# Conditioned residual block on one core: masks in a ring of six slots, and the second step's x tiles spread over 32 matrices

## Chip, core and metric

The kernel runs on one core of one Trainium2 chip. The metric is the device time of one execution in microseconds (us); the time of a kernel is the median of its runs. All arithmetic is on 32-bit floats. TensorE products are made three times, in split form (high and low parts), so that they come out near full precision.

## What is computed

```python
# x: 8 x 256 x 1024, mask: 8 x 1024 x 1024 of 0 and 1, W: 1024 x 1024
output = jnp.einsum('bsi,oi->bso', x, W) + b
sign = (2 * mask - 1)
diff = jnp.einsum('bsi,bio->bso', x, sign)
x = x + output + diff * coeff[:, None, None]
# then a gated feed-forward layer with low-rank adapters chosen by an index for each batch,
# down(silu(gate(x)) * up(x)), and x = x + that
```

The first part (here: stage 0) is what the change touches. For each of the 8 batches it is one product of x with a matrix of its own: W + identity + coeff * (2 * mask - 1). The feed-forward layer takes the other seven eighths of the time.

## The kernel before

**Steps and matrices.** The batches are handled in two steps s (`BLOCKS`) of four. In stage 0 the 1024 outputs are eight row tiles o, and each pair (batch b of four, row tile o) has one matrix of 128 x 1024. That is 64 matrices, numbered m = 0 to 63 here (`chunks`), and TensorE does 24 matmuls on each (`stage0`, L1245 to L1261): eight k tiles times three parts (high x high, high x low, low x high). Two matrices fill one bank of PSUM, and the bank is one tile q of 128 x 512 of the result.

**How a matrix is made.** SP loads its mask (`mask_dma`, L421) into `m_raw`, a ring of `S_RING` = 4 slots of 512 KB. ScalarE turns it into signs times coeff in place (`sign`, L638 to L643). VectorE adds the tile of W (`form_matrix`, L899 to L908), to which it has once for each row tile added the identity (L905). ScalarE rounds the sum into `m_hi` (`matrix_hi`, L645), VectorE puts the remainder into `m_lo` (`matrix_lo`, L910), and both are rings of four slots as well. A mask is loaded into a slot again when `matrix_lo` of four matrices earlier is done. `matrix_hi(m)` waits until TensorE is done with matrix m - 4.

**How x is made.** x is 32 tiles of 128 x 512, each split by ScalarE into a high part (`x_hi`) and by VectorE into a low part (`x_lo`). The 16 tiles of step 0 go to places of their own (`x_first`) at the start. The 16 tiles of step 1 (j = 16 to 31) go through `x_in`, a ring of `XIN_RING` = 4 slots, while step 0 is computed.

**Queues.** The order on each engine is written out by hand, as a loop over m with one body for each engine:

- SP (L475 to L481): the tile of W if m opens a row tile (`w_dma`, two slots, waits for the last matrix of the row tile before last), then mask m, then for m = 8 to 23 one x tile of step 1.
- ScalarE (L841 to L849), here "iteration m": for odd m the eviction of the finished tile (`finish_x1`), `sign(m + 5)`, `matrix_hi(m + 4)`, and for m = 2 to 17 `x_hi` of one tile of step 1.
- VectorE (L1178 to L1184), iteration m: `form_matrix(m + 5)`, `matrix_lo(m + 4)`, and for m = 2 to 17 `x_lo` of the same tile.
- GpSimd stores each finished tile of x1 to memory (L565 to L567), from a ring of three.

Each waits in its order, so what is behind a late `x_hi` on ScalarE is late too, and VectorE's next step with it.

**Start.** Masks 0 to 3 have slots free at once. Masks 4 to 7 are issued behind the 16 tiles of `x_first`. ScalarE and VectorE put matrix 4's sign and sum between the splits of tiles 11 and 12.

**Order of the row tiles.** Step 0 takes the halves of row tiles 0 and 1 in the order (0, 0), (1, 0), (0, 1), (1, 1), so that TensorE can go on before the second half of x has come. Step 1 takes them as (0, 0), (0, 1), (1, 0), (1, 1). Stage 0 ends when TensorE has done matrix 63; SP's loads of x1 for the next stage wait for that.

Of the kernel before, what the change touches and what calls it, by code (L numbers as in the profile page):

```python
# [7 lines left out]
P = 128  # L8
B, S, H, F, ADAPTERS, RANK = 8, 256, 1024, 2752, 16, 16
LORA_SCALE = 0.5  # L10
BLOCKS, HALVES = 2, 2
N = HALVES * S
HT = H // P
# [9 lines left out]
TR = 3 * R2  # L23
DR = 2 * RANK

S_RING = 4
G_RING, D_RING = 4, 8
G_RAW, D_RAW = 7, 14
OT_RING, FX_RING, LW_RING, X1_RING, XIN_RING = 3, 6, 2, 3, 4

PRODUCTS = ["p1", "p5", "p6", "p3", "p7", "p2", "p4"]
FIRST_PRODUCTS = ["p1", "p2", "p5", "p6", "p3", "p7", "p4"]
# [10 lines left out]

def first_stage_order():

    tiles = [(0, o, h) for o, h in [(0, 0), (1, 0), (0, 1), (1, 1)] + [(o, h) for o in range(2, HT) for h in range(2)]]
    return tiles + [(1, o, h) for o in range(HT) for h in range(2)]


def pe_order():  # L50
# [96 lines left out]
def build(nc, x, mask, coeff, w0, bias, wgu, wgu_half, wd, wd_left, a_gu, a_down, b_gu, b_down, idx, ident, own,  # L147
# [16 lines left out]
    with ExitStack() as ctx:  # L164
        def sb(stack, name, shape, dt):
            return stack.enter_context(nc.sbuf_tensor(name, shape, dt))
# [4 lines left out]
        def sems(name, n):  # L171
            return [sem(f"{name}{i}") for i in range(n)]
# [11 lines left out]

        with ExitStack() as first:
            xs = [sb(first, f"xs{s}", [P, HT * 2, 2 * N], f32r) for s in range(BLOCKS)]
            m_raw = sb(first, "m_raw", [P, S_RING, H], f32)
            m_hi = sb(first, "m_hi", [P, S_RING, H], f32r)
            m_lo = sb(first, "m_lo", [P, S_RING, H], f32r)
            w_in = sb(first, "w_in", [P, 2, H], f32)  # L190
            x_in = sb(first, "x_in", [P, XIN_RING, N], f32)
            x1_out = sb(first, "x1_out", [P, X1_RING, N], f32)
# [81 lines left out]
        x0_loaded, x_loaded = sems("x0_loaded", 2 * HT), sems("x_loaded", XIN_RING)  # L274
        xh_ready, xl_ready = sem("xh_ready"), sem("xl_ready")
        w_loaded, w_ident = sems("w_loaded", 2), sem("w_ident")
        m_loaded = sems("m_loaded", S_RING)
        sign_ready, m_ready, m_hi_ready, m_lo_ready = sem("sign_ready"), sem("m_ready"), sem("m_hi_ready"), sem("m_lo_ready")
        x1_made = sem("x1_made")
        x1_stored = sems("x1_stored", X1_RING)  # L280
# [130 lines left out]
        def _(sp):  # L411
            def x_dma(j):
                s, h, k = j // (2 * HT), j // HT % 2, j % HT
                if j < 2 * HT:
                    sp.dma_start(x_first[:, j, :], x[s, h, k, :, :]).then_inc(x0_loaded[j], 16)
                    return
                n = j - 2 * HT
                if n >= XIN_RING:
                    sp.wait_ge(xl_ready, j - XIN_RING + 1)
                sp.dma_start(x_in[:, n % XIN_RING, :], x[s, h, k, :, :]).then_inc(x_loaded[n % XIN_RING], 16)  # L420

            def mask_dma(m):
                s, o, b = chunks[m]
                if m >= S_RING:
                    sp.wait_ge(m_lo_ready, m - S_RING + 1)
                sp.dma_start(m_raw_i[:, m % S_RING, :], mask[4 * s + b, o, :, :]).then_inc(m_loaded[m % S_RING], 16)

            def w_dma(w):
                if w >= 2:
# [42 lines left out]
            mask_dma(3)  # L472
            for j in range(HT, 2 * HT):
                x_dma(j)
            for m in range(S_RING, len(chunks)):  # L475
                s, o, b = chunks[m]
                if s * HT + o >= 2 and b == 0:
                    w_dma(s * HT + o)
                mask_dma(m)
                if 8 <= m < 8 + 2 * HT:  # L480
                    x_dma(2 * HT + m - 8)  # L481

            sp.wait_ge(pe_done, done["s", first_half_end])
            for s in range(BLOCKS):
# [149 lines left out]
        def _(act):  # L634
            def copy(o, i):
                return nc.scalar.activation(o, i, ACT.Copy)  # L636

            def sign(m):  # L638
                s, o, b = chunks[m]
                act.wait_ge(m_loaded[m % S_RING], 16 * (m // S_RING + 1))  # L640
                nc.scalar.activation(m_raw[:, m % S_RING, :], m_raw_i[:, m % S_RING, :], ACT.Identity,
                                     bias=ncoeff[:, 4 * s + b:4 * s + b + 1], scale=coeff2[:, 4 * s + b:4 * s + b + 1]
                                     ).then_inc(sign_ready, 1)  # L643

            def matrix_hi(m):  # L645
                act.wait_ge(m_ready, m + 1)
                if m >= S_RING:
                    act.wait_ge(pe_done, done["s", m - S_RING])
                copy(m_hi[:, m % S_RING, :], m_raw[:, m % S_RING, :]).then_inc(m_hi_ready, 1)

            def x_hi(j):
                s, h, k = j // (2 * HT), j // HT % 2, j % HT
                if s == 0:
                    act.wait_ge(x0_loaded[j], 16)
                    src = x_first[:, j, :]
                else:
                    n = j - 2 * HT
                    if n == 0:
                        act.wait_ge(xl_ready, 2 * HT)
                    act.wait_ge(x_loaded[n % XIN_RING], 16 * (n // XIN_RING + 1))  # L660
                    src = x_in[:, n % XIN_RING, :]
                copy(xs[s][:, 2 * k, h * N:(h + 1) * N], src).then_inc(xh_ready, 1)
# [178 lines left out]
            for m in range(len(chunks)):  # L841
                if m % 2:
                    finish_x1(m // 2)
                if m + 5 < len(chunks):
                    sign(m + 5)
                if m + 4 < len(chunks):
                    matrix_hi(m + 4)
                if 2 <= m < 2 + 2 * HT:
                    x_hi(2 * HT + m - 2)  # L849

                if m == len(chunks) - 3:
                    for key in plan.items[:G_RING]:
                        prep(key)
# [35 lines left out]
        def _(dve):  # L889
            def sub(o, a, b):  # L890
                return nc.vector.tensor_tensor(o, a, b, ALU.subtract)  # L891

            def add(o, a, b):
                return nc.vector.tensor_tensor(o, a, b, ALU.add)  # L894
# [4 lines left out]
            def form_matrix(m):  # L899
                s, o, b = chunks[m]  # L900
                w = s * HT + o
                if b == 0:
                    dve.wait_ge(w_loaded[w % 2], 16 * (w // 2 + 1))
                    tile = w_in[:, w % 2, o * P:(o + 1) * P]
                    add(tile, tile, ident_sb[:, :]).then_inc(w_ident, 1)  # L905
                    dve.wait_ge(w_ident, w + 1)
                dve.wait_ge(sign_ready, m + 1)
                add(m_raw[:, m % S_RING, :], m_raw[:, m % S_RING, :], w_in[:, w % 2, :]).then_inc(m_ready, 1)  # L908

            def matrix_lo(m):  # L910
                dve.wait_ge(m_hi_ready, m + 1)
                sub(m_lo[:, m % S_RING, :], m_raw[:, m % S_RING, :], m_hi[:, m % S_RING, :]).then_inc(m_lo_ready, 1)

            def x_lo(j):
                s, h, k = j // (2 * HT), j // HT % 2, j % HT
                dve.wait_ge(xh_ready, j + 1)
                src = x_first[:, j, :] if s == 0 else x_in[:, (j - 2 * HT) % XIN_RING, :]
                cols = slice(h * N, (h + 1) * N)
                sub(xs[s][:, 2 * k + 1, cols], src, xs[s][:, 2 * k, cols]).then_inc(xl_ready, 1)
# [258 lines left out]
            for m in range(len(chunks)):  # L1178
                if m + 5 < len(chunks):
                    form_matrix(m + 5)  # L1180
                if m + 4 < len(chunks):
                    matrix_lo(m + 4)
                if 2 <= m < 2 + 2 * HT:
                    x_lo(2 * HT + m - 2)  # L1184

                if m == len(chunks) - 3:
                    make_first(plan.groups[0])
                    for key in plan.items[:G_RING]:
                        prep(key)
# [44 lines left out]
        def _(pe):  # L1234
# [10 lines left out]
            def stage0(m):  # L1245
                s, o, b = chunks[m]
                q, slot = m // 2, m % S_RING
                if m % 2 == 0 and q >= 4:
                    pe.wait_ge(x1_made, q - 3)
                pe.wait_ge(m_lo_ready, m + 1)  # L1250
                cols, dst = slice(b * S, (b + 1) * S), ps[q % 4][:, m % 2 * S:(m % 2 + 1) * S]
                for k in range(HT):
                    if (s, o) == (0, 0) or m == chunk_at[s, 0, 0]:
                        pe.wait_ge(xl_ready, 2 * HT * s + HT * (1 if s else b // 2) + k + 1)
                    elif (s, o, b) == (1, 0, 2) and k == 0:
                        pe.wait_ge(xl_ready, 4 * HT)
                    w = slice(k * P, (k + 1) * P)
                    mm(dst, m_hi[:, slot, w], xs[s][:, 2 * k, cols], start=k == 0, stop=False)  # L1258
                    mm(dst, m_hi[:, slot, w], xs[s][:, 2 * k + 1, cols], start=False, stop=False)  # L1259
                    end = mm(dst, m_lo[:, slot, w], xs[s][:, 2 * k, cols], start=False, stop=k == HT - 1)  # L1260
                end.then_inc(pe_done, 1)  # L1261
# [204 lines left out]
```

## Time and profile before

| | |
|---|---|
| median of three runs | 1719.38 us (1717.9 to 1721.31) |
| profiled execution, its own time | 1717.66 us |
| its span | 1715.9 us |
| TensorE matmul busy | 1586.7 us, 92% of the span |
| VectorE busy | 1284.7 us, 75% |
| ScalarE busy | 780.2 us, 45% |
| DMA, mean over the span | 190 GB/s, 325.23 MB |
| chain that ended last, by engine | PE 80%, DVE 8%, DMA 6%, ACT 2%, the rest 4% |

PE is TensorE, PEld its weight loads, DVE VectorE, ACT ScalarE, POOL GpSimd, SP the engine that issues most transfers. The engines' numbers are busy time within one profiled execution. The chain is followed back from the last instruction, at each step to what released it. Stage 0 is the first 217 us of the span, where TensorE's matmuls are those of L1258 to L1260.

### The profile page before, as it was taken

What the parts mean: (1) busy time and instruction counts of PE and PEld (TensorE: products, weight loads), DVE (VectorE), ACT (ScalarE), POOL (GpSimd) and SP (SyncE); (2) the same over time, 40 slices, a digit from 0 to 9 for tenths busy, and PEclk for the clock granted to TensorE, in tenths of its full rate; (3) what the DMA queues carried; (4) which work ended last, traced back from release to release, by engine and by line L of the source; (5) the groups of instructions that cost most, each with busy time, mean ns of one, the idle gap of its engine ahead of it and who ended that gap; (6) DMA issues with size and microseconds to landing.
All of it is one profiled execution on the core that took longest, in us unless ns stands there. A gap on an engine that the chain in (4) does not pass through costs nothing.

```text
span 1715.9 us, 23054 instructions
## 1 busy us (share of the span) xinstructions
PE 1586.7 (92%) x7502; PEld 1322.9 (77%) x7502; DVE 1284.7 (75%) x2250; ACT 780.2 (45%) x1426; POOL 344.2 (20%) x653
## 2 busy tenths in 40 slices
PE   6899948999999999969999579999999999699995
PEld 6899936888888888758888458888888888488884
DVE  7888857777777777668888877777677777688886
ACT  7888744444444444423333344444444444233321
POOL 0010121222222222161201011222222221511100
PEclk9999979999999999989999889999999999899998
DMA  8887672444444444698752734444444445996622
GB/s 302 295 281 278 239 235 95 144 145 144 145 144 145 144 145 144 198 397 282 249 200 74 246 113 133 146 146 149 144 147 146 147 144 164 379 335 230 224 65 98
DMA packets 134662, 325.23 MB, mean 190 GB/s; under 512 B 19216, under 2 KB 41872, under 8 KB 134544
## 3 DMA queue, kind: packets, MB, share of 16 engines
q0 software_dynamic: 58528, 188.39, 32.6%
q1 hardware_dynamic: 76016, 135.37, 23.9%
q8 instruction: 61, 1.00, 0.2%
q14 instruction: 57, 0.47, 0.1%
HBM read 231.42 MB, written 92.27 MB: 189 GB/s over the span
## 4 chain that ended last, share of the span: by engine, by line
PE 80%; DVE 8%; DMA 6%; ACT 2%; issue 2%; SPq 1%; POOL 1%; DVEq 0%; ACTq 0%; POOLq 0%
PE ps L1243 41%; PE ps L1239 28%; PE ps L1258 2%; PE ps L1260 2%; PE ps L1259 2%; PE ps L1346 2%; DMA fx<-x_scratch 2%; DMA x_in<-in_x 2%; DMA op_d<-operand_scratch 1%; DVE lo L891 1%; DVE acc L894 1%; DVE op_b L891 1%; DVE m_raw L894 1%; DVE m_lo L891 1%; DMA m_raw<-in_mask 1%
## 5 line engine op out<-in xcount | busy, mean ns | idle before, releaser
L636 ACT ACTIVATE hi<-raw 128x512 fp32r<-128x512 f32 (+1 forms) x598 | 309.4, 519 | 310.6 <-PE ps L1243 177.0
L1243 PE MATMUL ps<-op_b,hi 128*128 128x512 f32 x1360 | 422.1, 392 | 8.0 <-ACT u2c L636 6.2
L891 DVE TENSOR_TENSOR lo<-raw,hi 128x512 fp32r<-128x512 f32 (+2 forms) x646 | 338.5, 531 | 110.1 <-ACT hi L636 108.6
L1239 PE MATMUL ps<-op_b,hi 128*128 128x512 f32 x1056 | 333.6, 398 | 18.8 <-DVE op_b L891 18.8
L1243 PEld LDWEIGHTS ps<-op_b,hi 128*128 128x128 f32 x1360 | 256.6, 189 | 64.4 <-ACT u2c L636 7.1
L1243 PE MATMUL ps<-op_b,lo 128*128 128x512 f32 x680 | 266.8, 392 | 0.0
L894 DVE TENSOR_TENSOR acc<-acc,ps 128x512 f32<-128x512 f32 x312 | 212.1, 685 | 70.6 <-PE ps L1243 39.5
L1239 PEld LDWEIGHTS ps<-op_b,hi 128*128 128x128 f32 x1056 | 202.2, 192 | 64.4 <-issue 18.2
L1243 PE MATMUL ps<-op_d,hi 128*128 128x512 f32 x640 | 206.3, 404 | 29.5 <-DVE acc L894 28.3
L518 POOL DMA_DIRECT2D operand_scratch<-ot x140 | 75.5, 539 | 665.9 <-DVE ot L891 659.3
L1239 PE MATMUL ps<-op_b,lo 128*128 128x512 f32 x528 | 208.4, 395 | 0.0
L1258 PE MATMUL ps<-xs,m_hi 128*128 128x256 f32 x512 | 149.5, 292 | 23.3 <-DVE m_lo L891 22.0
L1243 PEld LDWEIGHTS ps<-op_d,hi 128*128 128x128 f32 x640 | 119.8, 193 | 64.3 <-DVE acc L894 38.4
L531 POOL DMA_DIRECT2D b_in<-in_b_gu x264 | 134.5, 510 | 94.0 <-DVE lw L891 74.2
L1239 PE MATMUL ps<-op_d,hi 128*128 128x512 f32 x480 | 149.2, 392 | 1.0 <-DMA op_d<-operand_scratch 0.8
L891 DVE TENSOR_TENSOR ot<-a,ot 128x512 fp32r<-128x512 f32 x124 | 85.5, 690 | 85.3 <-ACT ot L636 85.3
L1243 PEld LDWEIGHTS ps<-op_b,lo 128*128 128x128 f32 x680 | 128.4, 189 | 27.1
L1260 PE MATMUL ps<-xs,m_lo 128*128 128x256 f32 x512 | 148.1, 289 | 0.0
L1259 PE MATMUL ps<-xs,m_hi 128*128 128x256 f32 x512 | 148.1, 289 | 0.0
L891 DVE TENSOR_TENSOR raw<-raw 128x512 f32<-128x512 f32 (+1 forms) x246 | 137.1, 557 | 3.0
L1243 PE MATMUL ps<-op_d,lo 128*128 128x512 f32 x320 | 127.5, 398 | 0.0
L1258 PEld LDWEIGHTS ps<-xs,m_hi 128*128 128x128 f32 x512 | 101.5, 198 | 25.1 <-DVE m_lo L891 22.5
(120 smaller groups left out, 2232.8 us busy)
## 6 DMA issues: line engine op xcount, KB each, us to landing
operand_scratch<-ot POOLq DMA_DIRECT2D x140, 512.0 KB, 3.9
op_d<-operand_scratch POOLq DMA_DIRECT2D x140, 512.0 KB, 11.2
raw<-in_wgu SPq DMA_DIRECT2D x168, 256.0 KB, 4.1
m_raw<-in_mask SPq DMA_DIRECT2D x64, 512.0 KB, 4.7
raw<-in_wd SPq DMA_DIRECT2D x160, 128.0 KB, 4.2
fx<-x_scratch SPq DMA_DIRECT2D x64, 256.0 KB, 3.8
b_in<-in_b_gu POOLq DMA_DIRECT2D x264, 32.0 KB, 2.3
w_in<-in_w SPq DMA_DIRECT2D x16, 512.0 KB, 4.8
```

Of the source, the lines that this page charges most:

```text
L518: pool.dma_start(dst, ot[:, 2 * slot:2 * slot + 2, :].rearrange("p a n -> p (a n)")).then_inc(ot_stored[slot], 16)
L531: pool.dma_start(b_in[c % 2][r:r + RANK, b // 2 * 2:b // 2 * 2 + 2, :], b_gu[ds(adapter[b], 1), :, :, 2 * P * c:2 * P * (c + 1)].rearrange ...
L636: return nc.scalar.activation(o, i, ACT.Copy)
L891: return nc.vector.tensor_tensor(o, a, b, ALU.subtract)
L894: return nc.vector.tensor_tensor(o, a, b, ALU.add)
L1239: return mm(dst, weight, v, start=start, stop=stop)
L1243: return mm(dst, weight, v, start=False, stop=stop, skip_group_check=True)
L1258: mm(dst, m_hi[:, slot, w], xs[s][:, 2 * k, cols], start=k == 0, stop=False)
L1259: mm(dst, m_hi[:, slot, w], xs[s][:, 2 * k + 1, cols], start=False, stop=False)
L1260: end = mm(dst, m_lo[:, slot, w], xs[s][:, 2 * k, cols], start=False, stop=k == HT - 1)
L1346: end = mm(ps[6 + half][:, :], lw_ap(key, half), ot[:, i, :], start=f == 0 and i == slot, stop=False)
```

## The change

Five edits, all in stage 0:

1. `m_raw` gets a ring of its own, `M_RING` = 6, so a mask is loaded when `matrix_lo` of six matrices earlier is done. `m_hi` and `m_lo` stay at four.
2. `XIN_RING` goes from 4 to 2.
3. The x tiles of step 1 are loaded after every second mask (m = 8, 10, .. 38) and split in every second iteration (m = 2, 4, .. 32).
4. At the start mask 4 is issued between the `x_first` tiles 11 and 12, mask 5 behind tile 15; the loop begins at mask 6.
5. Step 1 takes its first two row tiles in the same interleaved order as step 0, and TensorE waits for x tile by tile in the first matrix of each half of a row tile 0.

```diff
-S_RING = 4
+S_RING, M_RING = 4, 6
-OT_RING, FX_RING, LW_RING, X1_RING, XIN_RING = 3, 6, 2, 3, 4
+OT_RING, FX_RING, LW_RING, X1_RING, XIN_RING = 3, 6, 2, 3, 2
@@ def first_stage_order():
-    tiles = [(0, o, h) for o, h in [(0, 0), (1, 0), (0, 1), (1, 1)] + [(o, h) for o in range(2, HT) for h in range(2)]]
-    return tiles + [(1, o, h) for o in range(HT) for h in range(2)]
+    tiles = [(0, 0), (1, 0), (0, 1), (1, 1)] + [(o, h) for o in range(2, HT) for h in range(2)]
+    return [(s, o, h) for s in range(BLOCKS) for o, h in tiles]
@@
-            m_raw = sb(first, "m_raw", [P, S_RING, H], f32)
+            m_raw = sb(first, "m_raw", [P, M_RING, H], f32)
@@ mask_dma (sign, matrix_hi, form_matrix and matrix_lo use m % M_RING for m_raw likewise)
-                if m >= S_RING:
-                    sp.wait_ge(m_lo_ready, m - S_RING + 1)
+                if m >= M_RING:
+                    sp.wait_ge(m_lo_ready, m - M_RING + 1)
@@ SP's order
             for j in range(HT, 2 * HT):
                 x_dma(j)
-            for m in range(S_RING, len(chunks)):
+                if j == HT + 3:
+                    mask_dma(4)
+            mask_dma(5)
+            for m in range(M_RING, len(chunks)):
                 s, o, b = chunks[m]
                 if s * HT + o >= 2 and b == 0:
                     w_dma(s * HT + o)
                 mask_dma(m)
-                if 8 <= m < 8 + 2 * HT:
-                    x_dma(2 * HT + m - 8)
+                if m % 2 == 0 and 0 <= m - 8 < 4 * HT:
+                    x_dma(2 * HT + (m - 8) // 2)
@@ ScalarE's loop (VectorE's likewise, with x_lo)
-                if 2 <= m < 2 + 2 * HT:
-                    x_hi(2 * HT + m - 2)
+                if m % 2 == 0 and 0 <= m - 2 < 4 * HT:
+                    x_hi(2 * HT + (m - 2) // 2)
@@ stage0 on TensorE
-                    if (s, o) == (0, 0) or m == chunk_at[s, 0, 0]:
-                        pe.wait_ge(xl_ready, 2 * HT * s + HT * (1 if s else b // 2) + k + 1)
-                    elif (s, o, b) == (1, 0, 2) and k == 0:
-                        pe.wait_ge(xl_ready, 4 * HT)
+                    if o == 0 and b % 2 == 0:
+                        pe.wait_ge(xl_ready, 2 * HT * s + HT * (b // 2) + k + 1)
```

## Rows read from the trace of the kernel before

**Rows 1.** TensorE's matmuls in time: start, us, operation, idle before it and releaser

```profile
31.52 0.39 PE L1258 MATMUL ps<-xs,m_hi 128*128 128x256 f32 x1 [3.17 <-DVE m_lo L891]
...
42.99 0.39 PE L1258 MATMUL ps<-xs,m_hi 128*128 128x256 f32 x1 [1.09 <-DVE m_lo L891]
...
57.50 0.39 PE L1258 MATMUL ps<-xs,m_hi 128*128 128x256 f32 x1 [2.68 <-DVE m_lo L891]
...
72.06 0.39 PE L1258 MATMUL ps<-xs,m_hi 128*128 128x256 f32 x1 [2.69 <-DVE m_lo L891]
...
96.10 0.35 PE L1258 MATMUL ps<-xs,m_hi 128*128 128x256 f32 x1 [0.55 <-DVE m_lo L891]
...
214.25 0.28 PE L1258 MATMUL ps<-xs,m_hi 128*128 128x256 f32 x1
```

**Rows 2.** Waits from 28 to 98 us, TensorE's then ScalarE's: total, times, longest

```profile
PE ps L1258 <- DVE m_lo L891: 11.4, 6, 3.2
...
ACT xs L636 <- DMA x_in<-in_x: 12.7, 6, 3.6
```

**Rows 3.** Busy time by stretch: PE, PEld, DVE, ACT, POOL; then PEclk, DMA share, GB/s

```profile
32.00:34.00 2.00, 2.00 (x12) 2.00 (x11) 2.00 (x3) 2.00 (x3) 0.00 (x0) 0.50 0.84 291
44.00:54.00 10.00, 10.00 (x85) 10.00 (x85) 8.24 (x10) 7.27 (x11) 0.54 (x1) 1.00 0.96 346
56.00:58.00 2.00, 0.50 (x4) 0.50 (x5) 2.00 (x4) 2.00 (x3) 0.00 (x0) 1.00 0.06 23
43.00:101.00 58.00, 50.81 (x401) 50.02 (x402) 49.10 (x53) 48.65 (x58) 4.86 (x9) 0.97 0.80 282
101.00:145.00 44.00, 44.00 (x369) 44.00 (x368) 36.82 (x36) 37.51 (x40) 3.78 (x7) 1.00 0.81 280
```

**Rows 4.** ScalarE in time, from 53 to 57 us

```profile
53.18 0.67 ACT L669 ACTIVATE x_out<-ps,bias_sb 128x512 f32<-128x512 f32 x1
53.75 1.23 ACT L641 ACTIVATE m_raw<-m_raw,ncoeff,coeff 128x1024 f32<-128x1024 int32 x1
54.88 1.04 ACT L636 ACTIVATE m_hi<-m_raw 128x1024 fp32r<-128x1024 f32 x1
55.83 0.62 ACT L636 ACTIVATE xs<-x_in 128x512 fp32r<-128x512 f32 x1
56.35 1.23 ACT L641 ACTIVATE m_raw<-m_raw,ncoeff,coeff 128x1024 f32<-128x1024 int32 x1
```

**Rows 5.** VectorE in time, from 58 to 61 us

```profile
57.96 1.22 DVE L894 TENSOR_TENSOR m_raw<-m_raw,w_in 128x1024 f32<-128x1024 f32 x1
59.10 1.22 DVE L891 TENSOR_TENSOR m_lo<-m_raw,m_hi 128x1024 fp32r<-128x1024 f32 x1
60.23 0.69 DVE L891 TENSOR_TENSOR xs<-x_in,xs 128x512 fp32r<-128x512 f32 x1
60.84 1.22 DVE L894 TENSOR_TENSOR m_raw<-m_raw,w_in 128x1024 f32<-128x1024 f32 x1
```

**Rows 6.** VectorE's group for W plus identity, first 217 us: busy, mean ns

```profile
L894 DVE TENSOR_TENSOR w_in<-w_in,ident_sb 128x128 f32<-128x128 f32 x16 | 4.6, 285 | 3.9 <-DMA ident_sb<-in_ident 3.9
```

**Rows 7.** Transfers to landing: masks' median of stage 0, `x_in` min/median/max

```profile
m_raw<-in_mask SPq DMA_DIRECT2D x64, 512.0 KB, 4.7
...
DMA to landing us min/median/max: 3.8/5.5/6.5
```

**Rows 8.** The start in time, from 24 to 39 us: ScalarE, VectorE, SP, ScalarE

```profile
24.28 1.25 ACT L641 ACTIVATE m_raw<-m_raw,ncoeff,coeff 128x1024 f32<-128x1024 int32 x1 [1.03 <-DMA m_raw<-in_mask]
...
25.55 1.23 DVE L894 TENSOR_TENSOR m_raw<-m_raw,w_in 128x1024 f32<-128x1024 f32 x1 [0.73 <-ACT m_raw L641]
...
30.35 0.33 SPq L431 DMA_DIRECT2D w_in<-in_w  x1
...
31.86 0.43 SPq L420 DMA_DIRECT2D x_in<-in_x  x1
...
38.13 0.63 ACT L636 ACTIVATE xs<-x_in 128x512 fp32r<-128x512 f32 x1 [3.58 <-DMA x_in<-in_x]
```

More of the change, by code:

```diff
@@ L276, in build @@
         w_loaded, w_ident = sems("w_loaded", 2), sem("w_ident")
-        m_loaded = sems("m_loaded", S_RING)
+        m_loaded = sems("m_loaded", M_RING)
         sign_ready, m_ready, m_hi_ready, m_lo_ready = sem("sign_ready"), sem("m_ready"), sem("m_hi_ready"), sem("m_lo_ready")
@@ L423, in mask_dma @@
                 s, o, b = chunks[m]
-                if m >= S_RING:
-                    sp.wait_ge(m_lo_ready, m - S_RING + 1)
-                sp.dma_start(m_raw_i[:, m % S_RING, :], mask[4 * s + b, o, :, :]).then_inc(m_loaded[m % S_RING], 16)
+                if m >= M_RING:
+                    sp.wait_ge(m_lo_ready, m - M_RING + 1)
+                sp.dma_start(m_raw_i[:, m % M_RING, :], mask[4 * s + b, o, :, :]).then_inc(m_loaded[m % M_RING], 16)
             def w_dma(w):
@@ L639, in sign @@
                 s, o, b = chunks[m]
-                act.wait_ge(m_loaded[m % S_RING], 16 * (m // S_RING + 1))
-                nc.scalar.activation(m_raw[:, m % S_RING, :], m_raw_i[:, m % S_RING, :], ACT.Identity,
+                act.wait_ge(m_loaded[m % M_RING], 16 * (m // M_RING + 1))
+                nc.scalar.activation(m_raw[:, m % M_RING, :], m_raw_i[:, m % M_RING, :], ACT.Identity,
                                      bias=ncoeff[:, 4 * s + b:4 * s + b + 1], scale=coeff2[:, 4 * s + b:4 * s + b + 1]
@@ L648, in matrix_hi @@
                     act.wait_ge(pe_done, done["s", m - S_RING])
-                copy(m_hi[:, m % S_RING, :], m_raw[:, m % S_RING, :]).then_inc(m_hi_ready, 1)
+                copy(m_hi[:, m % S_RING, :], m_raw[:, m % M_RING, :]).then_inc(m_hi_ready, 1)
             def x_hi(j):
@@ L907, in form_matrix @@
                 dve.wait_ge(sign_ready, m + 1)
-                add(m_raw[:, m % S_RING, :], m_raw[:, m % S_RING, :], w_in[:, w % 2, :]).then_inc(m_ready, 1)
+                add(m_raw[:, m % M_RING, :], m_raw[:, m % M_RING, :], w_in[:, w % 2, :]).then_inc(m_ready, 1)
             def matrix_lo(m):
                 dve.wait_ge(m_hi_ready, m + 1)
-                sub(m_lo[:, m % S_RING, :], m_raw[:, m % S_RING, :], m_hi[:, m % S_RING, :]).then_inc(m_lo_ready, 1)
+                sub(m_lo[:, m % S_RING, :], m_raw[:, m % M_RING, :], m_hi[:, m % S_RING, :]).then_inc(m_lo_ready, 1)
             def x_lo(j):
@@ L1182, in _ @@
                     matrix_lo(m + 4)
-                if 2 <= m < 2 + 2 * HT:
-                    x_lo(2 * HT + m - 2)
+                if m % 2 == 0 and 0 <= m - 2 < 4 * HT:
+                    x_lo(2 * HT + (m - 2) // 2)
                 if m == len(chunks) - 3:
```

## The prediction

> **What bounds the kernel now.** I read the windows first, to see where TensorE is not full in stage 0; then its matmuls in time, for the first one behind each gap; then the waits of TensorE and of what releases it; last the order on ScalarE and VectorE. TensorE is full from 101 us on (369 matmuls in 44 us, clock 1.00) but not from 43 to 101 us (50.81 of 58 us busy, clock 0.97) [rows 3]. So the place to look is the first 101 us, where the second step's x tiles are loaded and split. Behind a gap stand the matmuls at 31.52, 42.99, 57.50, 72.06 and 96.10 us (and one at 86.6 us); they open matrices 4, 7, 11, 15, 22 and 19 [rows 1]. All were released by `matrix_lo`, 11.4 us in six waits [rows 2]. VectorE was late because ScalarE was, and ScalarE stood still 12.7 us in six waits for an `x_in` tile [rows 2]. The reader should see a period: about 14.5 us from gap to gap (42.99, 57.50, 72.06), which is four matrices, and every fourth matrix brings a tile of W.
>
> Why is an x tile late, when its ring has four slots? Not for lack of slots. SP issues it behind its mask, and mask m waits for `matrix_lo(m - 4)`, which VectorE does in iteration m - 8. ScalarE needs the tile in iteration m - 6. Two iterations are 5.8 us, and the tile takes 3.8 to 6.5 us to land, 5.5 at the median [rows 7]; with W's 512 KB ahead it is always at the long end.
>
> The full pace: matrices 22 to 63 start from 96.10 to 214.25 us [rows 1], 118.15 / 41 = 2.882 us each. From matrix 7 (42.99) to matrix 63 (214.25) it takes 171.26 us, where 56 matrices at full pace are 161.4. That leaves **9.9 us** to be had behind matrix 7: four gaps, plus matmuls at half clock behind one of them.
>
> **Masks in six slots.** Mask m now waits for `matrix_lo(m - 6)`, in iteration m - 10, and `sign(m)` is in iteration m - 5: five iterations, 14.4 us, against a median landing of 4.7 us [rows 7]. The x tile behind it is issued in iteration m - 10 and needed in m - 6: four iterations, 11.5 us, against at most 6.5 us [rows 7]. The ring of two for `x_in` adds a wait: tile i waits for `x_lo` of tile i - 2, which is also in iteration m - 10, just behind the `matrix_lo` that the mask waited for. Queued behind that wait on SP are only later masks, themselves not due for four iterations or more. It costs nothing, as long as a landing takes less than four iterations. `w_dma` ahead of mask m waits for the sum of matrix m - 5, also in iteration m - 10, so it holds up nothing either.
>
> **Splits over 32 matrices.** Start to start, ScalarE's steps are 0.57 (eviction), 1.13 (sign), 0.95 (high part), 0.52 (x) [rows 4]; VectorE's are 1.14 (sum), 1.13 (low part), 0.61 (x) [rows 5], and 0.285 for W once in four [rows 6]. Four matrices before: ScalarE 4 x (1.13 + 0.95 + 0.52) + 2 x 0.57 = 11.5, VectorE 4 x 2.88 + 0.3 = 11.8; TensorE needs 4 x 2.882 = 11.5. So both were at TensorE's pace or over it even with no transfer late, and could never catch up. After: ScalarE 11.5 - 2 x 0.52 = 10.5, VectorE 11.8 - 2 x 0.61 = 10.6. They gain 0.9 us on TensorE in each four matrices. Matrices 18 to 33, which had no split and now have one in two, keep this margin, so the added work there is hidden by TensorE; if that cover were gone it would cost at most 8 x 0.61 = 4.9 us.
>
> **DMA.** In four matrices go four masks and a W tile of 0.524 MB each, two stores of x1 (0.524 MB together) and now two x tiles (0.524 MB) for four: 3.67 MB in 11.53 us, 318 GB/s. The trace moved 346 GB/s over the ten busy us from 44 to 54, and 23 GB/s from 56 to 58, while TensorE had nothing [rows 3]. The mean of 282 over 43 to 101 us therefore holds idle stretches and is no ceiling. I take 346 as the nearest row for what the queue can do, and keep 282 for a rival. More of SP's transfers are now in flight beside GpSimd's stores, which have three slots and so 17 us each; I cost that at nothing.
>
> The Trainium skill's page "DMA: Bandwidth & Descriptors" (section "Issuing engines are not separate DMA queues") says that transfers of all issuing engines run on the same 16 DMA engines and interleave. That speaks against a deeper ring, since masks sent early delay the x tiles and the stores. The trace agrees so far as the `x_in` tile takes up to 6.5 us behind other transfers against 3.8 at its shortest. Taken at its worst it is the first rival below.
>
> **The start.** ScalarE waited 1.03 us for mask 4 and VectorE then 0.73 us for ScalarE [rows 8]. With mask 4 issued four tiles earlier both waits go; the bytes up to tile 15 are the same, so that tile comes when mask 4 came before (24.3 us), and it is split near 26 us. VectorE has no other slack, so everything is 0.73 us earlier: matrix 4 at 30.8 instead of 31.52. The gap ahead of it stays over 2 us. Next late is the first `x_in` tile. Its W tile was issued at 30.35, itself at 31.86, and it was there at 38.13 us [rows 8]. W now goes at 29.6; mask 8 no longer waits for `matrix_lo(4)`, so the x tile goes at 30.35. By bytes from W (7.8 us) it lands at 37.4, by its own issue (6.2 to 6.3 us) at 36.6: 0.7 to 1.5 us earlier than before, I take 1.1. From 38.13 to matrix 7 at 42.99 the chain is unchanged, so matrix 7 starts at 41.9. TensorE itself would be ready at 42.99 - 1.09 - 0.16 (the modelled end) - 0.73 = 41.0 us; matrix 7 keeps a gap of about 1 us. From there `matrix_lo(8)` is some 0.5 us ahead of TensorE, and the lead grows by 0.2 us for each matrix.
>
> **Interleaving in step 1.** Row tiles 0 and 1 of step 1 now share the two W slots for eight matrices. W of row tile 1 goes ahead of mask 34 instead of 36 and waits for the sum of matrix 31, in iteration 26, where mask 34 alone would have gone in iteration 24. Behind it on SP stand mask 34, an x tile due in iteration 28, and mask 35. From W to x took 7.8 us at the start [rows 8], here some two iterations are to be had, so ScalarE may wait about 2 us there once. But `matrix_lo(m + 4)` is then four matrices ahead of TensorE, some 4.6 us of slack, so I cost it at nothing; without that cover it is 2 us. The next one (W ahead of mask 40, waiting for the sum of matrix 37) has no x tile behind it. TensorE's tile-by-tile waits on x find it split: tile 31 is due in iteration 32, the first user is matrix 36.
>
> **The sum.** 9.9 (behind matrix 7) + 1.1 (ahead of it) = 11.0 us. Stage 0 ends 11.0 us sooner, and what follows starts from TensorE's last matrix and GpSimd's last store, both moved alike; nothing later is touched. 1717.66 - 11.0 = 1706.7 us for the profiled execution. That one is 1.7 us under the median of the runs, so the median is **1708.4 us**. Unknown are the landing of the first tile (0.4 either way) and the clock. Behind the gap of 3.17 us the clock was 0.50 [rows 3], behind one of 2.68 it was 1.00, behind one of 2.69 half again (that matrix took 4.3 us instead of 2.8). Now there may be two short gaps, before matrices 4 and 7; a clock that falls before matrix 7 costs 1.5 us more.
>
> The page "TensorE: Matmul & The Clock Gate" (section "Part 1: The HAM clock gate") says that idling sends the engine back to the low clock and busy time brings it up again. The trace agrees for 3.17 us; for the shorter gaps it shows both. If any gap did it, 1.5 us of the 11.0 would go.
>
> **Rivals.** First: DMA becomes the bound in matrices 8 to 39. At 282 GB/s [rows 3] four matrices take 13.0 us instead of 11.53, eight times 1.5 is 11.9 us, and the sum is 11.0 - 11.9: 1720.3 us, no change. At 310 GB/s it is 8 x 0.3 = 2.4 us, 1710.8; at 300, 8 x 0.7 = 5.6, 1714. For it speaks the demand, 92% of the 346 of a busy stretch; against it the idle stretch at 56 us and the stretch from 101 to 145 us, full with 280 GB/s at a DMA share of 0.81 [rows 3]. Six per cent for the range 1711 to 1715, five for no change.
>
> Second, and slower: the ring of two ties the x tiles into a loop. `x_lo` of tile i - 2, the issue, the landing L, `x_hi` and `x_lo` of tile i: two x tiles, that is four matrices, in about L + 1.4 us. It decides from L = 10.1 us (11.53 - 1.4). At L = 12.5 the four matrices take 13.9 us, eight times 2.4 is 19, and the time 1727. The largest landing of `x_in` is 6.5 us [rows 7], and the change takes load off the queue. Four per cent.
>
> Third: the gaps don't go but get smaller, because something of the chain that the profile doesn't show (a semaphore's way, the order of ScalarE and VectorE in lock step) eats the margin of 0.2 us for each matrix. Half of 9.9 us stays: 1713. Five per cent.
>
> **How the numbers follow.** Forecast 80%: 1708.4, with its own bounds 1706 to 1711. The runs before scatter by 1.5 to 1.9 us about the median; the range 1705 to 1714 takes in the forecast with that, the clock and the mild cases of rivals one and three. A measurement of this kernel can tell about 0.2% (3.4 us) from no change. Faster by more than that: 80 + 6 + 5 = 91%; within it 5%; slower 4%.
>
> **What the profile will show.** Right: first matmul of matrix 4 near 30.8, of matrix 7 near 41.9 us, then no gap to the last, whose matrix 63 starts near 203.3 us; ScalarE's waits for `x_in` down from 12.7 to about 2 us at the first tile and up to 2 at matrix 34's; a DMA rate near 318 GB/s from 45 to 130 us. Wrong: gaps at matrices 11, 15, 19 that come back with DMA share near 1 (first rival), SP waiting long for `x_lo` (second), or small gaps at each matrix with DMA below its rate (third). A later stage that is longer or shorter by more than 2 us would be something I have not seen.

## The result, and the profile after

The changed kernel takes 1702.59 us, the median of four runs (1700.69 to 1705.56), beside 1718.64 us for the kernel before; the ratio is 0.9912, with the interval 0.9897 to 0.9927. Timed again with six more runs it took 1705.35 us beside 1717.87 us (ratio 0.9922, 0.9905 to 0.9939). The forecast was 1708.4 us with the range 1705 to 1714. The gaps went as forecast; the gain came out larger, and the recorded median lies 2.4 us below the range.

First the windows of the changed kernel that answer to [rows 3] (stretch, busy time of PE, PEld, DVE, ACT, POOL, then granted clock, DMA share, GB/s):

```profile
43.00:101.00 58.00, 58.00 (x485) 58.00 (x485) 56.99 (x60) 56.83 (x65) 5.90 (x11) 1.00 0.92 335
101.00:145.00 44.00, 44.00 (x369) 44.00 (x368) 38.23 (x39) 38.45 (x43) 4.32 (x8) 1.00 0.85 303
```

From 43 to 101 us TensorE is now full: 485 matmuls where there were 401. The transfers moved 335 GB/s in place of 282. Over the longer stretch from 45 to 130 us they moved 315 GB/s, where 318 was forecast. The first matmuls of matrices 4 and 7, and of matrix 63, answer to [rows 1]:

```profile
30.72 0.39 PE L1259 MATMUL ps<-xs,m_hi 128*128 128x256 f32 x1 [1.98 <-DVE m_lo L894]
...
41.05 0.39 PE L1259 MATMUL ps<-xs,m_hi 128*128 128x256 f32 x1 [1.44 <-DVE m_lo L894]
...
202.43 0.28 PE L1259 MATMUL ps<-xs,m_hi 128*128 128x256 f32 x1
```

These two gaps are the only ones from matrix 4 on; those ahead of matrices 11, 15, 19 and 22 are gone. From matrix 7 to matrix 63 it is 202.43 - 41.05 = 161.4 us, which is the full pace, where it was 171.26. Matrix 63 starts 11.8 us sooner. ScalarE's row for mask 4, which had 1.03 us of idle time in [rows 8], and its two waits for an `x_in` tile in this kernel:

```profile
23.17 1.23 ACT L644 ACTIVATE m_raw<-m_raw,ncoeff,coeff 128x1024 f32<-128x1024 int32 x1
...
36.20 0.63 ACT L639 ACTIVATE xs<-x_in 128x512 fp32r<-128x512 f32 x1 [2.76 <-DMA x_in<-in_x]
...
109.26 0.63 ACT L639 ACTIVATE xs<-x_in 128x512 fp32r<-128x512 f32 x1 [2.58 <-DMA x_in<-in_x]
```

There is no wait for mask 4, one of 2.8 us for the first tile, and one of 2.6 us for the tile that stands behind the early W tile ahead of mask 34. In all they are 5.3 us, against 12.7.

The span is 1698.9 us, 17.0 less than before. Stage 0 brings 11.8 of that. The other 5.2 us lie behind stage 0, where not one instruction is changed. That is the question for the experiments.

### The profile page after: what moved, and what is told of

It is laid out like the page before. It is cut to its first block, busy times and chain, and to the rows that moved or that the text cites. A ratio compares the mean times of both kernels' runs of the same rounds, so it can differ in the third digit from the quotient of the medians.

```text
span 1698.9 us, 23052 instructions
## 1 busy us (share of the span) xinstructions
PE 1579.1 (93%) x7502; PEld 1315.5 (77%) x7502; DVE 1283.6 (76%) x2250; ACT 778.4 (46%) x1426; POOL 344.3 (20%) x653
## 4 chain that ended last, share of the span: by engine, by line
PE 82%; DVE 8%; DMA 4%; issue 2%; ACT 2%; POOL 1%; SPq 0%; DVEq 0%; ACTq 0%; POOLq 0%
PE ps L1246 41%; PE ps L1242 28%; PE ps L1259 3%; PE ps L1261 3%; PE ps L1260 3%; PE ps L1347 2%; DMA fx<-x_scratch 2%; DVE lo L894 2%; DVE acc L897 1%; DMA op_d<-operand_scratch 1%; DVE op_b L894 1%; DVE fx L894 1%; DMA m_raw<-in_mask 0%; PE ps L1326 0%; DVE raw L894 0%
## 5 line engine op out<-in xcount | busy, mean ns | idle before, releaser
L1259 PE MATMUL ps<-xs,m_hi 128*128 128x256 f32 x512 | 147.5, 288 | 15.6 <-DVE m_lo L894 14.3
L1246 PEld LDWEIGHTS ps<-op_b,lo 128*128 128x128 f32 x680 | 128.1, 188 | 27.1
L1260 PE MATMUL ps<-xs,m_hi 128*128 128x256 f32 x512 | 146.7, 287 | 0.0
L1242 PEld LDWEIGHTS ps<-op_b,lo 128*128 128x128 f32 x528 | 100.8, 191 | 22.4
```

What stands on the lines that cost most here:

```text
L1242: return mm(dst, weight, v, start=start, stop=stop)
L1246: return mm(dst, weight, v, start=False, stop=stop, skip_group_check=True)
```

## Experiments

A ratio below is to the kernel before, timed beside the run. That kernel took 1717.87 us (23 runs) beside the first timing of both kernels again, "Slots alone" and "Spreading alone", and 1716.71 us (11 runs) beside the other four variants. So ratios are compared here, not times. All variants but the two unedited kernels have one profile each.

### Both kernels again, unedited

> The kernel before, unchanged, timed against itself. Theory A (the 5 us beyond my forecast lie behind stage 0 and come from when TensorE's clock happens to be low at the borders of the stages, anew in each execution): the ratio is 1.000 within its interval, the runs scatter by 4 to 6 us, and in the profile the time from the last matmul of stage 0 to the end of the span, 1498.9 us in the profile before, differs by 1 to 4 us with no edit at all, all of it at the borders (near 220 to 290, 730 to 770, 960 to 1020, 1470 to 1500 us). Theory B (the change makes the later stages shorter): this time is again 1498.9 within 1 us.

> The changed kernel, unchanged, with more rounds. Theory A: matrix 63 starts again at 202.4 within 0.5 us, the time from there to the end is not again 1493.7 but somewhere from 1493 to 1499 us, and the median gain over the kernel before is 12 to 14 us (ratio 0.992 to 0.993). Theory B: the later stages take 1493.7 within 1 us again and the gain is 16 to 17 us (ratio 0.990 to 0.991).

> The kernel before once more, for a further profile. Theory A (chance at the borders): the time behind the last matmul of stage 0 is again 1497 to 1501 us, and stage 0 itself ends between 217 and 219.5 us, according to how long the clock is low behind its gaps (6.8 us of low clock in the first profile, 10.2 in the second). Theory B (the first profile of the changed kernel shows a real gain behind stage 0): all profiles of this one lie above 1498, all of the changed kernel at 1494.

> The changed kernel once more, for a further profile. Theory A: stage 0 ends at 205.3 within 0.5 us, with no low clock behind its two short gaps, and the time behind it lies anywhere from 1494 to 1501 us. Theory B: 1494 within 1 us.

> As the last one of the kernel before: stage 0 ends between 217 and 219.5 us, the rest takes 1497 to 1501 us by theory A.

> As the last one of the changed kernel: stage 0 ends at 205.3 within 0.5 us, the rest takes anywhere from 1494 to 1501 us by theory A, 1494 by theory B.

The kernel before against itself gave a ratio of 0.9998 (0.9985 to 1.0011), its own 12 runs from 1713.38 to 1723.06 us, which is 9.7 us where 4 to 6 were expected. Where stage 0 ends is read from the start of its last matmul, the second number of "first and last start" in the rows of the line (durations min/median/max in ns ahead of it). In the order changed kernel first profile, second profile, kernel before second profile:

```profile
L1261 PE MATMUL ps<-xs,m_lo x512: 278/283/415, 11.5 to 205.2; 128*128 128x256 f32 x171
```

```profile
L1261 PE MATMUL ps<-xs,m_lo x512: 279/283/415, 11.6 to 205.4; 128*128 128x256 f32 x171
```

```profile
L1260 PE MATMUL ps<-xs,m_lo x512: 278/283/420, 11.8 to 219.1; 128*128 128x256 f32 x171
```

| profile | stage 0 ends | span | from there to the end |
|---|---|---|---|
| before, 1st | 217.0 | 1715.9 | 1498.9 |
| before, 2nd (`same_before`) | 219.1 | 1717.2 | 1498.1 |
| before, 3rd | 218.0 | 1715.5 | 1497.5 |
| before, 4th | 217.6 | 1716.5 | 1498.9 |
| changed, 1st | 205.2 | 1698.9 | 1493.7 |
| changed, 2nd (`same_after`) | 205.4 | 1706.1 | 1500.7 |
| changed, 3rd | 205.8 | 1705.9 | 1500.1 |
| changed, 4th | 205.9 | 1703.1 | 1497.2 |

Theory B falls by the changed kernel: the same program takes 1493.7 and 1500.7 us behind stage 0. The second profile of the kernel before, 1498.1 against 1498.9, would by itself have fitted theory B, and 1500.7 lies above the 1493 to 1499 that theory A gave. The means are 1498.4 and 1497.9 us. No gain shows there, and the changed kernel's first profile was one that came out short with nothing changed. Stage 0 itself ends at 217.95 us in the mean of four and at 205.57 us, so its gain is 12.4 us, not 11.8 and not 17. The median of 1705.35 against 1717.87 us, 12.5 us, agrees.

The chance sits at the borders of the stages, as theory A had it. These are the four borders, each from one matmul to the same other matmul of the program, first in the first profile of the changed kernel, then in its second (the same columns as above):

```profile
205.20:265.00 59.80, 32.53 (x104) 23.05 (x102) 40.84 (x72) 27.61 (x52) 17.76 (x33) 0.80 0.63 201
701.50:736.20 34.70, 25.93 (x102) 19.13 (x100) 20.49 (x47) 10.85 (x28) 24.73 (x43) 0.90 1.04 366
927.90:1008.70 80.80, 52.80 (x201) 40.21 (x200) 69.22 (x136) 35.69 (x66) 10.63 (x20) 0.83 0.56 187
1442.70:1484.20 41.50, 27.08 (x102) 20.30 (x102) 25.87 (x54) 12.84 (x31) 21.62 (x38) 0.86 1.07 380
```

```profile
205.40:268.30 62.90, 34.25 (x105) 24.64 (x103) 40.76 (x72) 27.67 (x52) 17.75 (x33) 0.78 0.61 191
704.80:740.40 35.60, 26.99 (x101) 19.92 (x100) 20.41 (x47) 10.86 (x28) 25.62 (x45) 0.86 1.05 368
933.60:1015.80 82.20, 53.28 (x202) 40.50 (x201) 69.19 (x136) 35.62 (x66) 10.63 (x20) 0.83 0.56 184
1449.70:1491.70 42.00, 27.76 (x101) 21.21 (x100) 25.66 (x54) 12.84 (x31) 21.60 (x38) 0.82 1.07 376
```

The same work takes 59.8 and 62.9 us, 34.7 and 35.6, 80.8 and 82.2, 41.5 and 42.0: 216.8 against 222.7 us, 5.9 of the 7.0 us between the two. Here TensorE waits often and its clock is at the lower level for a part of the time. In the third and fourth profile of the changed kernel the borders add up to 221.3 and 218.2 us, in the four of the kernel before to 221.5, 221.7, 220.6 and 221.7. The matmuls that start in them while the granted clock is 0.50, counted in the trace, number 92 in the first and 113 in the second profile of the changed kernel. Over all 14 profiles of this study such counts and the time of the borders go together only in part (correlation 0.73). So the place of most of the scatter is shown. That the clock is a part of its cause is likely from this, but no run shows it, and the rest is open.

### Slots alone

> Masks in five slots, everything else as before: x tiles of step 1 in four slots, one in each of 16 matrices, the start and the order of step 1 untouched (six slots beside four x slots don't fit the memory, five do). Masks and x tiles are issued three iterations ahead of their use instead of two to three. Theory: the waits for the x_in tile go but for the first, VectorE stays at 11.8 us for four matrices against TensorE's 11.53 and the transfers at 355 GB/s, so small gaps stay from matrix 8 to 23: 8 to 9 us of the gain, matrix 63 near 206 us, 1710. Rival (the spreading is what brings it, the slots little): gaps of 2 us and more at matrices 11, 15, 19 stay, gain under 4 us.

```diff
-S_RING = 4
+S_RING, M_RING = 4, 5
 # m_raw, its semaphores and mask_dma by M_RING; all else as before, XIN_RING = 4
```

Measured: 1708.08 us, ratio 0.9936 (0.9914 to 0.9958). Stage 0 ends at 208.1 us, matrix 63 starts at 205.3. One gap is left behind matrix 7, ahead of matrix 19. Its row, and the window over the stretch with the x tiles:

```profile
78.44 0.39 PE L1258 MATMUL ps<-xs,m_hi 128*128 128x256 f32 x1 [0.72 <-DVE m_lo L891]
```

```profile
43.00:101.00 58.00, 57.28 (x472) 56.66 (x471) 57.11 (x61) 56.72 (x67) 5.93 (x11) 1.00 0.94 332
```

So the longer lead brings most of the gain: 217.95 - 208.06 = 9.9 us of stage 0 with x still split in 16 matrices, and 9.2 of it behind matrix 7 (165.79 us from there to the end of the stage, where the kernel before took 174.98 in the mean). The rival falls. With five slots the x tile has three iterations where it had two, and the mask has four where it had three. The expectation gives three to both. VectorE is busy 57.11 of 58 us here, which is the bound that was forecast (11.8 us for four matrices). Up to matrix 20 the low part of a matrix is done only 0.15 us before TensorE's first matmul on it, so TensorE goes at VectorE's pace. What wasn't run is the x tile issued ahead of its mask, with four slots of each; in the first profile of the kernel before ScalarE waited for no mask between 28 and 98 us, so that order might have given much of this with no slot more.

### Spreading alone

> The x tiles of step 1 over 32 matrices with the interleaved order that this needs, but masks in four slots as before and x_in in four. Theory: each x tile is still issued only two iterations before its use, with a W tile ahead of every second one. The loop of landing (6.4), ScalarE's eviction and sign, VectorE's sums and low parts takes about 13.6 us for four matrices, against 14.5 before, but now eight times instead of four: 109 us from matrix 7 to 39 against 102 before, so no gain or up to 6 us slower, 1719 to 1725, with gaps of 1.5 to 2.5 us at every fourth matrix up to 39. Rival (spreading takes the load off ScalarE, VectorE and the queue, and the gaps go): 5 to 10 us faster.

```diff
-                if 8 <= m < 8 + 2 * HT:
-                    x_dma(2 * HT + m - 8)
+                if m % 2 == 0 and 0 <= m - 8 < 4 * HT:
+                    x_dma(2 * HT + (m - 8) // 2)
 # likewise x_hi and x_lo, and the order of step 1; M_RING = S_RING = 4, XIN_RING = 4
```

Measured: 1720.95 us, ratio 1.0012 (0.9998 to 1.0026): no gain, perhaps a loss. There are gaps at every fourth matrix from 11 to 27 and then ahead of 33, 35, 37 and 39, the last ones from 0.17 to 1.0 us; these are the rows ahead of matrices 11, 15, 19, 23, 27 and 33, and then ScalarE's waits for an `x_in` tile from 28 to 160 us (total, times, longest):

```profile
55.61 0.39 PE L1256 MATMUL ps<-xs,m_hi 128*128 128x256 f32 x1 [0.81 <-DVE m_lo L891]
...
68.73 0.39 PE L1256 MATMUL ps<-xs,m_hi 128*128 128x256 f32 x1 [1.35 <-DVE m_lo L891]
...
81.53 0.39 PE L1256 MATMUL ps<-xs,m_hi 128*128 128x256 f32 x1 [1.02 <-DVE m_lo L891]
...
95.00 0.38 PE L1256 MATMUL ps<-xs,m_hi 128*128 128x256 f32 x1 [1.37 <-DVE m_lo L891]
...
108.58 0.50 PE L1256 MATMUL ps<-xs,m_hi 128*128 128x256 f32 x1 [1.80 <-DVE m_lo L891]
...
128.62 0.39 PE L1256 MATMUL ps<-xs,m_hi 128*128 128x256 f32 x1 [1.01 <-DVE m_lo L891]
```

```profile
ACT xs L636 <- DMA x_in<-in_x: 20.7, 11, 3.4
```

The theory holds in kind: the gaps are about half as long and there are nine of them behind matrix 7 where there were four, since the tile is still late (11 waits, where the kernel before had six). In size it expected too much: the gaps are 0.2 to 1.8 us, not 1.5 to 2.5. The period up to matrix 27 is 12.8 to 13.6 us (81.53 - 68.73 = 12.8, 108.58 - 95.00 = 13.6), at most the 13.6 that was forecast, and matrices 7 to 39 took 104.9 us instead of 109. The rival, that spreading by itself frees ScalarE, VectorE and the queue, falls.

### Five slots and four x slots, with everything else of the change

> The changed kernel with masks in five slots instead of six and x_in in four instead of two (the same memory); spread, start and order as changed. Theory: three iterations of lead (8.6 us) for masks and x tiles are enough, since together with a W tile they land in 7.8; matrix 63 within 0.5 us of the changed kernel's 202.4 to 202.7, no new gap. Rival (the sixth slot is needed, or the ring of two costs something): gaps of 1 us and more come or go, matrix 63 differs by over 1 us.

```diff
-S_RING, M_RING = 4, 6
+S_RING, M_RING = 4, 5
-... XIN_RING = ..., 2
+... XIN_RING = ..., 4
-            mask_dma(5)
```

Measured: 1704.08 us, ratio 0.9923 (0.9903 to 0.9943); matrix 63 starts at 202.6 us and stage 0 ends at 205.4, as with six and two slots. ScalarE's waits for `x_in` are longer (8.1 us in five, against 5.3 in two), but none reaches TensorE. So neither the sixth slot is needed nor does the ring of two cost anything that shows. The stage ends at 208.1 with five slots, 219.9 with spreading, 205.4 with both. But the last also has the changed start, and 1.1 of the 2.7 us between it and five slots alone lie ahead of matrix 7 (41.1 against 42.3). Behind matrix 7 the stage takes 164.3 us against 165.8: spreading is worth about 1.5 us once the lead is there, and nothing without it.

### The start, and the order of step 1

> The changed kernel with the start undone: masks 4 and 5 behind the 16 x_first tiles again. Theory: ScalarE waits 1.0 us for mask 4 and VectorE 0.7, matrix 4 starts at 31.5 instead of 30.7 and everything to matrix 63 is 0.7 to 0.8 us later (203.2); if TensorE's clock falls behind the longer gap there is no more to lose, since matrix 7 waits for its low part anyway. In the total 0.8 us, less than can be told.

```diff
-                if j == HT + 3:
-                    mask_dma(4)
-            mask_dma(5)
-            for m in range(M_RING, len(chunks)):
+            for m in range(4, len(chunks)):
```

Measured: 1706.08 us, ratio 0.9933 (0.9910 to 0.9955); matrix 4 at 31.8 us, matrix 63 at 203.6, stage 0 ends at 206.4. Here the gap ahead of matrix 4 is 2.93 us and the clock fell behind it (0.79 over 30 to 38 us); matrix 7 had no gap left.

> The changed kernel with step 1's row tiles in the order of before: the second half of x is first used in matrix 34 instead of 36. Theory: no difference to speak of. The wait of 2.6 us of ScalarE for an x_in tile near 107 us, which the early W tile of row tile 1 brings, goes; instead TensorE waits up to 0.5 us in matrix 34 for the last x tile, whose low part is made 5 us after matrix 32 ends, while matrix 34 asks for it after 5.4. Matrix 63 within 0.7 us of 202.4. Rival (the interleaving is needed): a gap of over 1 us at matrix 34.

```diff
-    return [(s, o, h) for s in range(BLOCKS) for o, h in tiles]
+    # step 0 as changed, step 1 as (o, h) for o in range(HT) for h in range(2)
```

Measured: 1706.03 us, ratio 0.9932 (0.9911 to 0.9953); matrix 63 at 203.6 us, 1.2 us beyond 202.4 where 0.7 was allowed. From matrix 7 (42.2) to 63 it is again 161.4 us, so there is no gap at matrix 34 and the rival falls: the spreading doesn't need the interleaved order; ScalarE's wait near 109 us is gone, as expected. But matrix 4 starts at 31.8 us here too, although the start is as changed. ScalarE got its third mask 1.1 us later than in the profile of the changed kernel, and matrix 4 of the changed kernel itself lies between 30.7 and 31.5 us in four profiles. So the 0.8 us of the earlier mask 4 are seen only as the missing wait of ScalarE; in the time of the stage they are within its scatter, and this run doesn't settle what they are worth.

### One more edit: the first two x tiles sent at once

> The changed kernel with one more edit: masks 6 and 7 and the first two x_in tiles, whose slots have never been used, are issued right behind mask 5 at the start, instead of behind the W tile that waits for the sum of matrix 5. Theory: the 2.8 us that ScalarE waits for the first x_in tile go; the low part of matrix 7 is then due at 39.2 us (sign of matrix 8 waits about 1 us for its mask instead) and TensorE is ready at 39.5, so the gap of 1.6 us ahead of matrix 7 closes: matrix 63 starts at 200.9 instead of 202.4 us, total 1.5 us less than the changed kernel. Rival (ScalarE's wait is only passed on to mask 8 or the W tile, which now come behind the same landing): matrix 7 still near 41, no gain.

```diff
-            mask_dma(5)
-            for m in range(M_RING, len(chunks)):
+            for m in (5, 6, 7):
+                mask_dma(m)
+            for j in (2 * HT, 2 * HT + 1):
+                x_dma(j)
+            for m in range(M_RING + 2, len(chunks)):
@@
-                if m % 2 == 0 and 0 <= m - 8 < 4 * HT:
+                if m % 2 == 0 and 2 <= (m - 8) // 2 < 2 * HT:
```

ScalarE's row of the first `x_in` tile, then its sign of matrix 8, then TensorE's first matmul of matrix 7:

```profile
33.60 0.62 ACT L642 ACTIVATE xs<-x_in 128x512 fp32r<-128x512 f32 x1
...
35.68 1.25 ACT L647 ACTIVATE m_raw<-m_raw,ncoeff,coeff 128x1024 f32<-128x1024 int32 x1 [0.89 <-DMA m_raw<-in_mask]
...
39.72 0.28 PE L1262 MATMUL ps<-xs,m_hi 128*128 128x256 f32 x1
```

The tile is there in time, 0.9 us of the wait passes to mask 8, and matrix 7 follows without a gap. Matrix 63 starts at 201.0 us (forecast 200.9), stage 0 ends at 203.8, 1.8 us sooner than the mean of the changed kernel. In the whole, 1704.84 us and a ratio of 0.9932 (0.9915 to 0.9948) can't be told from the changed kernel's 0.9922.

## Why the prediction was right and wrong

**What bounds it.** Right. The late `x_in` tile was due to its lead of two iterations, not its slots: with one mask slot more and the same four x slots the gaps ahead of matrices 11, 15 and 22 go and that ahead of matrix 19 shrinks to 0.7 us; with half the x tiles per matrix and no longer lead there are still gaps. Of the five edits, the lead brings 9.2 us behind matrix 7 and the spreading about 1.6. Ahead of matrix 7 the changed kernel gains 1.5 us, of which five slots alone, with the old start, show 0.7 in their one profile.

**9.9 us behind matrix 7.** In the pair of profiles it is 171.26 - 161.4 = 9.9 us, as worked out. It is the term that was under-sized all the same, because I read it from one execution. In four profiles of the kernel before, matrix 7 starts at 42.97 us in the mean and the stage ends 174.98 us later; in the changed kernel it is 41.43 and 164.14 us. That is 10.8 us. What differs among the four are the gaps themselves, and the matmuls behind them at half clock: one of the gaps ahead of matrices 11, 15 and 19 was followed by low clock in each profile, but not always the same one. In the second it was matrix 11's, whose gap of 2.68 us in [rows 1] had no such end (first the matmul behind the gap, then a window about it):

```profile
57.63 0.39 PE L1258 MATMUL ps<-xs,m_hi 128*128 128x256 f32 x1 [2.86 <-DVE m_lo L891]
```

```profile
52.00:64.00 12.00, 9.14 (x64) 8.93 (x63) 9.63 (x12) 10.89 (x14) 1.08 (x2) 0.86 0.73 262
```

**1.1 us ahead of matrix 7.** Measured 1.9 in the first pair (42.99 to 41.05), 1.5 in the means. The W tile and the first x tile were issued at 29.56 and 30.40 us, as forecast (29.6 and 30.35). The x tile was there at 36.2 us, below both of my ends (36.6 and 37.4), and at 36.4, 36.8 and 36.9 us in the other three profiles, 36.6 in the mean. So it is the end by its own issue that held; I had taken a value between the two. From W's issue to the x tile's landing the transfers moved 299 GB/s, where the kernel before moved 277; why is not shown.

**Masks in six slots, ring of two, W tiles at nothing.** Right for the masks and the ring of two: SP waits for `x_lo` only 6.5 us in all from 28 to 160 us, and TensorE sees none of it. For the W tiles it is wrong once. "`w_dma` ahead of mask m waits for the sum of matrix m - 5" doesn't hold ahead of mask 8, where it waits for matrix 5, three earlier, because the row tiles are interleaved there. That W tile holds up the first x tile. With masks 6 and 7 and two x tiles issued ahead of it, the gap ahead of matrix 7 was gone and stage 0 ended 1.8 us sooner. The sum doesn't suffer, as "The start" took W at its real time.

**Margin of 0.9 us in four matrices.** Right. In the changed kernel's first profile the low part of matrices 8, 12, 16, 20 and 24 is done 0.76, 1.62, 2.52, 3.42 and 4.33 us before TensorE's first matmul on it: 0.9 us more in each four. From matrix 28 on it is at most 4.8 us, and ScalarE waits for TensorE at its evictions.

**DMA.** The demand of 318 GB/s was met (315 from 45 to 130 us); the rate was above it, 335, while the lead was being built, and 303 from 101 to 145 us. Masks now take 5.8 us to land at the median instead of 4.7, with more transfers in flight. The lead of 14.4 us hides that. The first rival falls with the ceiling of 282 GB/s on which it rested. The 346 GB/s that I took for the queue was too low as well. The trace of the kernel before had a stretch against it at the start (the first row), where masks and the x tiles of step 0 stood in the queue; the changed kernel has another (the second row):

```profile
12.00:22.00 10.00, 8.69 (x41) 8.10 (x40) 9.58 (x12) 8.71 (x12) 0.00 (x0) 1.00 1.05 392
```

```profile
34.00:44.00 10.00, 8.56 (x71) 8.36 (x71) 7.46 (x10) 7.80 (x10) 1.09 (x2) 1.00 1.03 415
```

Against 392 GB/s the demand of 318 is 81%, not 92%, so the first rival had less for it than I gave it.

**Interleaving.** The wait of about 2 us once on ScalarE was there, 2.6 us at 109 us, and hidden as worked out.

**The clock.** I held a low clock behind the two short gaps possible, for 1.5 us. In none of the four profiles of the changed kernel was it low in stage 0 from matrix 4 on, while the four of the kernel before had 6.8 to 10.2 us of it there.

**The base and the range: the step that failed.** Direction and mechanism were right; what failed is the size of terms of the sum, and the range. The largest is "that one is 1.7 us under the median of the runs", the step from 1706.7 to 1708.4. It rests on a median of three runs, 1719.38. Twenty-three runs of the same kernel gave 1717.87, so the profiled execution (1717.66) was 0.2 us under the median, and that term was 1.5 us too large. The two terms of the gain came to 11.0 us and measured 12.4: 10.84 for the 9.9 behind matrix 7, 1.54 for the 1.1 ahead of it. Base and terms together are 1.5 + 1.4 = 2.9 of the 5.8 us from 1708.4 to 1702.59. Corrected by them the forecast would have been 1705.5, and six more runs of the same program gave 1705.35.

The other 2.9 us are the four executions of the result, which came out low with nothing changed. For the one of them that was profiled the trace shows where: 1493.7 us behind stage 0 instead of a mean of 1498. For the other three it isn't known. The range left 3.4 us below the forecast, about what base and terms used up. It took 1.5 to 1.9 us of scatter from three runs, whereas executions of this kernel lie over 9.7 us (1713.38 to 1723.06). So that the result fell outside the range, rather than near its lower end, was in part chance. "A later stage shorter by more than 2 us would be something I have not seen": it was seen, and it was no effect of the change that the means show.

## What to carry to other kernels

When a transfer in a ring is late, count the iterations from the event that lets it be issued to its use, and hold them against the landing time with all that is queued ahead; a slot more in the ring that gates the queue can be worth more than the load that is taken off it. Spreading work over more steps helps only once the lead is there; without it the same late arrival comes more often. Before a gain is ascribed to a stage that was not touched, profile both kernels a second time, and take the base and the scatter for the range from many executions, not from three. For what the queue can do, look through the whole trace for its fullest stretch, not only near the place of the change.

## What the runs showed of the hardware that I had not expected

The same program took from 1493.7 to 1500.7 us for the same instructions behind stage 0. Of those 7.0 us 5.9 were at the four borders between stages, where TensorE waits and its clock is at 1.2 GHz for a part of the time; the long stretch of 434 us between the third and the fourth border agrees within 1.2 us over all profiles.

Of the gaps ahead of a matrix in stage 0 from matrix 4 on, in 14 profiles, all eight of 2.9 us and more were followed by the 1.2 GHz level (2.93 to 3.84 us). Those from 1.8 to 2.9 us were followed by it five times (1.80, 2.60, 2.61, 2.69, 2.86) and ten times not (1.80, 1.94, 1.98, 1.99, 2.12, 2.47, 2.63, 2.68, 2.69, 2.71). None under 1.8 us was. So the length of the gap alone doesn't decide it. The one of 1.80 us with low clock behind it stood ahead of matrix 27 with spreading alone:

```profile
110.00:112.00 2.00, 2.00 (x11) 2.00 (x11) 2.00 (x3) 2.00 (x3) 0.54 (x1) 0.50 0.93 307
```

And the transfers moved 335 GB/s for 58 us and up to 415 over ten, where I had taken 346 over ten as the nearest to what the queue can do. At the start of the kernel before, the ten us at 392 GB/s were loads issued by SP alone.
